# Attention of a two-block sequence model on one core: 1024-column steps, maxima split on POOL and carried through DRAM, scores three steps ahead

## What is computed

```python
q, k, v = (qkv[:, :, 0], qkv[:, :, 1], qkv[:, :, 2])
scale = D ** (-0.5)
scores = jnp.einsum('blhd,bmhd->bhlm', q * scale, k)
attn = jax.nn.softmax(scores, axis=-1)
o = jnp.einsum('bhlm,bmhd->blhd', attn, v).reshape(b, l, c)
```

## Time and profile before

| | |
|---|---|
| runs | 3390.99 us median of 3 (3388.45 to 3393.36) |
| profiled execution, its own time | 3393.34 us |
| its span | 3391.6 us |
| granted PE clock, mean | 0.918 |
| busy: PE, DVE, ACT, POOL | 2929.7, 1827.1, 1464.5, 1628.7 us |
| attention, first `values` to last | 766.2 to 1991.3 us of the span |

### The profile page before, as it was taken

One profiled execution on the slowest core, in us unless ns is written; L12 is line 12 of the kernel. 1 busy time (PEld: TensorE's weight loads), 2 busy tenths in 40 slices (PEclk: granted clock), 3 DMA queues, 4 the chain that ended last, 5 costly groups with the idle time before them and its releaser, 6 DMA issues. The chain is left out here.

```text
span 3391.6 us, 53705 instructions
## 1 busy us (share of the span) xinstructions
PE 2929.7 (86%) x16130; PEld 2357.2 (70%) x16130; DVE 1827.1 (54%) x3056; ACT 1464.5 (43%) x2832; POOL 1628.7 (48%) x1401
## 2 busy tenths in 40 slices
PE   6759899978988889889898967757999999999976
PEld 2147778746656656666565646657999999999975
DVE  3446566568888888888888847760111111111125
ACT  2112222218888888888898842221111111111112
POOL 1232322118888878888888856881222222222210
PEclk8769899979999999999999977878999999999989
DMA  5366565552323323233232234659212112121134
GB/s 163 131 210 209 180 222 201 203 155 55 72 64 76 67 63 78 64 69 72 64 78 64 64 124 175 217 201 305 67 34 67 35 34 67 34 67 34 41 123 159
DMA packets 334756, 373.83 MB, mean 110 GB/s; under 512 B 162577, under 2 KB 226713, under 8 KB 334606
## 3 DMA queue, kind: packets, MB, share of 16 engines
q1 hardware_dynamic: 327128, 359.12, 35.4%
q10 hardware_dynamic: 7482, 12.69, 1.2%
HBM read 221.81 MB, written 149.36 MB: 109 GB/s over the span
## 5 line engine op out<-in xcount | busy, mean ns | idle before, releaser
L754 POOL TENSOR_TENSOR a_pl<-a_pf,a_ph 128x512 fp32r<-128x512 f32 x768 | 1038.4, 1384 | 218.6 <-ACT a_ph L829 218.4
L769 DVE TENSOR_REDUCE a_mx<-a_psum_s 128x1 f32<-128x1024 f32 x512 | 618.5, 1219 | 174.9 <-PE a_psum_s L860 170.1
L829 ACT ACTIVATE a_ph<-a_pf 128x512 fp32r<-128x512 f32 x1024 | 674.7, 659 | 0.0
L824 ACT ACTIVATE a_pf<-a_psum_t 128x512 f32<-128x512 f32 x1024 | 635.3, 621 | 55.1 <-PE a_psum_t L877 53.0
L1433 POOL TENSOR_TENSOR m_al<-m_af,m_ah 128x256 fp32r<-128x256 f32 x288 | 212.4, 737 | 769.2 <-DVE m_ah L1442 769.2
L1481 PE MATMUL m_psum_h<-m_ht,m_w 128*128 128x256 f32 x4032 | 534.8, 284 | 33.4 <-DMA m_w<-w_s 23.0
L1442 DVE CAST m_ah<-m_af 128x256 fp32r<-128x256 f32 x288 | 84.5, 293 | 841.2 <-ACT m_af L1419 841.2
L1481 PEld LDWEIGHTS m_psum_h<-m_ht,m_w 128*128 128x128 f32 x4032 | 509.1, 190 | 37.1 <-issue 35.9
L1495 PE MATMUL m_psum_y<-m_w,m_ah 128*128 128x288 f32 x2304 | 507.1, 297 | 1.4 <-DVE m_y L1459 1.2
L1419 ACT ACTIVATE m_af<-m_psum_h,m_bias 128x256 f32<-128x256 f32 x288 | 137.0, 476 | 818.5 <-PE m_psum_h L1481 818.5
L892 PE MATMUL a_psum_o<-a_ph,a_vs 128*100 128x512 f32 x1024 | 438.6, 428 | 37.9 <-DVE a_pl L802 31.1
(11 more groups left out here) (218 smaller groups left out, 3133.8 us busy)
## 6 DMA issues: line engine op xcount, KB each, us to landing
a_qs<-q_s SPq DMA_DIRECT2D x192, 144.0 KB
a_ks<-k_s SPq DMA_DIRECT2D x192, 144.0 KB
w_s<-q_ws SPq DMA_DIRECT2D x64, 324.0 KB, 3.4
h_s<-p_ht SPq DMA_DIRECT2D x40, 512.0 KB, 5.2
m_ht<-h_s SPq DMA_DIRECT2D x16, 1280.0 KB, 8.4
v_s<-q_vo SPq DMA_DIRECT2D x64, 288.0 KB, 2.3
a_vs<-v_s SPq DMA_DIRECT2D x128, 144.0 KB
q_s<-q_qko SPq DMA_DIRECT2D x32, 512.0 KB, 2.7
```

Of the source, the lines that this page charges most:

```text
L754: pool.tensor_tensor(pl[:, s % RING], pf[:, s % RING], raw(ph[:, s % RING]), ALU.subtract).then_inc(lo_pool, 1)
L769: dve.tensor_reduce(mx[:, u % 2, t:t + 1], p_s[:, bank(u, t)], AX.X, ALU.max) \
L824: act.activation(pf[:, s % RING], p_t[:, s % 2], ACT.Exp, scale=SCALE) \
L829: act.activation(ph[:, s % RING], pf[:, s % RING], ACT.Copy).then_inc(hi_ready, 1)
```

## The change

The attention works in 8 steps of 1024 columns for each head. ACT makes the exponential twice from PSUM (rounded to fp32r, and full), in place of once with a copy. The maxima are split on POOL without a turn, and two DMAs write them to DRAM, element by element; a third DMA reads them back as rows. The rows in `ks` are -1 now, so nothing is negated. `p_s` holds one tile, in place of two, `p_t` two tiles of 1024 columns. The transposed scores go three steps ahead. `finish` is in two parts, with a `max_tile` between them. DVE makes two low parts of 8, reading the full exponential in PSUM.

```diff
-    AHEAD = 5
+    PAIR = 2
+    STEPS = LH * KT // PAIR
+    PER_LH = STEPS // LH
+    COLS = PAIR * GT
+    AHEAD = 3
+    DVE_LO = (1, 5)
-        p_s = ps("s", [P, 2, L])
-        p_t = ps("t", [P, 2, GT])
+        p_s = ps("s", [P, L])
+        p_t = ps("t", [P, 2, COLS])
...
+                def send_max(hd, u):
+                    sp.wait_ge(mh_lo, hd + 1)
+                    for s in range(2):
+                        sp.dma_start(maxima[u, s].rearrange("(t c) -> c t", c=P), raw(mh[:, u % 2, s]),
+                                     allow_slow_non_contiguous=True).then_inc(max_out[u], 16)
                 def put_max(u, i):
-                    sp.wait_ge(s_free[bank(u, KT)], bank_uses(u, i, KT) + 1)
-                    for s in range(2):
-                        sp.dma_start(raw(qs[SROWS + s:SROWS + s + 1, u]).rearrange("o (t c) -> o t c", c=P),
-                                     raw(mxt[:, u % 2, s])).then_inc(max_in[u], 16)
+                    sp.wait_ge(max_out[u], 32 * (i + 1))
+                    sp.dma_start(raw(qs[SROWS:MROWS, u]), maxima[u]).then_inc(max_in[u], 16)
...
                 def body(hd, u, i, last):
                     if not (last and u > 0):
                         sp.wait_ge(p_free, RING + STEPS * hd)
                         load(hd + SLOTS - 1, (u + SLOTS - 1) % SLOTS)
                     if not (last and u == SLOTS - 1):
+                        send_max(hd + 1, (u + 1) % SLOTS)
                         put_max((u + 1) % SLOTS, i + (u + 1) // SLOTS)
...
+                def split_max(hd, u, puts):
...
+                    pool.tensor_copy(mh[:, u % 2, 0], mx[:, u % 2]).then_inc(mh_hi, 1)
+                    pool.wait_ge(mh_hi, hd + 1)
+                    pool.tensor_tensor(mh[:, u % 2, 1], mx[:, u % 2], raw(mh[:, u % 2, 0]), ALU.subtract) \
+                        .then_inc(mh_lo, 1)
...
-                dve.memset(raw(qs[:, 0]), 1.0).then_inc(first_set_up, 1)
...
+                    for k in range(1, STEPS + 1):
+                        over, s = divmod(k, STEPS)
+                        if not (last and u + over >= SLOTS - 2):
+                            max_tile(hd + over + 2, (u + over + 2) % SLOTS, s)
+                        if s + LO_AHEAD in DVE_LO and not (last and u + over == SLOTS):
+                            low(hd + over, s + LO_AHEAD)
+                        if s + LO_AHEAD - STEPS in DVE_LO and not (last and u == SLOTS - 1):
+                            low(hd + 1, s + LO_AHEAD - STEPS)
+                        if (s + 1) % PER_LH == 0:
+                            finish_hi(hd, s // PER_LH)
+                        if s % PER_LH == 0:
+                            finish_lo(hd, s // PER_LH - 1 if s else LH - 1)
...
+                        act.activation(ph[:, s % RING], p_t[:, s % 2], ACT.Exp, scale=SCALE)
+                        full = p_t[:, s % 2] if s in DVE_LO else pf[:, s % RING]
+                        act.activation(full, p_t[:, s % 2], ACT.Exp, scale=SCALE).then_inc(exp_done, 1)
...
+                    if not (isinstance(hd, int) and hd == 0 and t == 0):
+                        pe.wait_ge(s_free, KT * hd + t)
...
+                    if s >= 2 and s - 2 in DVE_LO:
+                        pe.wait_ge(lo_dve, lo_counts(hd, s - 2)[1])
+                    elif not (isinstance(hd, int) and hd == 0 and s < 2):
+                        pe.wait_ge(exp_done, STEPS * hd + s - 1)
...
                         values(hd, u, s)
                         if not (last and u >= SLOTS - 2):
-                            nxt = ((u + 2) % SLOTS, i + (u + 2) // SLOTS)
-                            if s in MAX_STEP:
-                                score_tile(*nxt, MAX_STEP.index(s))
-                            if s == TURN_STEP:
-                                turn(*nxt)
+                            score_tile(hd + 2, (u + 2) % SLOTS, i + (u + 2) // SLOTS, s)
```

More of the change, by code:

```diff
@@ L684, in heads @@
                 body(SLOTS * (n - 1) + u, u, n - 1, True)
[L686 to L692, removed]
         def lo_counts(n_heads, s):
-            d = sum(dve_lo(x) for x in range(s + 1))
+            d = sum(x <= s for x in DVE_LO)
             return NPOOL * n_heads + s + 1 - d, NDVE * n_heads + d
@@ L760, in _, with low, finish_hi, finish_lo @@
             def _(dve):
-                dve.memset(raw(qs[:, 0]), 1.0).then_inc(first_set_up, 1)
                 dve.memset(raw(vs[:, 0]), 1.0).then_inc(first_set_up, 1)
-                dve.memset(raw(qs[:, 1:SLOTS]), 1.0).then_inc(set_up, 1)
                 dve.memset(raw(vs[:, 1:SLOTS]), 1.0).then_inc(set_up, 1)
                 def max_tile(hd, u, t):
[L768 to L782, removed]
+                    if t == 0 and not (isinstance(hd, int) and hd < 2):
+                        dve.wait_ge(mh_lo, hd - 1)
+                    dve.wait_ge(s_ready, KT * hd + t + 1)
+                    dve.tensor_reduce(mx[:, u % 2, t:t + 1], p_s[:], AX.X, ALU.max).then_inc(s_free, 1)
+                def low(hd, s):
+                    dve.wait_ge(exp_done, STEPS * hd + s + 1)
+                    dve.tensor_tensor(pl[:, s % RING], p_t[:, s % 2], raw(ph[:, s % RING]), ALU.subtract) \
+                       .then_inc(lo_dve, 1)
+                def finish_hi(hd, lh):
+                    dve.wait_ge(p_free, RING + STEPS * hd + PER_LH * (lh + 1))
+                    dve.wait_ge(o_out[lh], START + 16 * STORES * hd)
                     dve.tensor_copy(ob[:, lh], p_o[0:VLO, lh]).then_inc(hi_copied, 1)
+                def finish_lo(hd, lh):
                     dve.wait_ge(hi_copied, LH * hd + lh + 1)
@@ L789, in _ @@
                         max_tile(hd, hd, t)
-                    if hd == 0:
-                        turn_lo(0, 0)
+                for s in DVE_LO:
+                    if s < LO_AHEAD:
+                        low(0, s)
+                max_tile(2, 2, 0)
                 def body(hd, u, i, last):
[L794 to L806, removed]
+                    for k in range(1, STEPS + 1):
[10 more added lines that the diff above has]
+                            finish_lo(hd, s // PER_LH - 1 if s else LH - 1)
                 heads(nc.vector, body)
@@ L812, in _ @@
                 set_start(act, o_out + max_in + o_copied)
[L813 to L832, removed]
                 def body(hd, u, i, last):
                     for s in range(STEPS):
[L837 to L844, removed]
+                        act.wait_ge(t_ready, STEPS * hd + s + 1)
+                        act.wait_ge(p_free, STEPS * hd + s + 1)
+                        act.activation(ph[:, s % RING], p_t[:, s % 2], ACT.Exp, scale=SCALE)
+                        full = p_t[:, s % 2] if s in DVE_LO else pf[:, s % RING]
+                        act.activation(full, p_t[:, s % 2], ACT.Exp, scale=SCALE).then_inc(exp_done, 1)
                 heads(nc.scalar, body)
@@ new lines, in scores @@
+                    if s >= 2 and s - 2 in DVE_LO:
+                        pe.wait_ge(lo_dve, lo_counts(hd, s - 2)[1])
+                    elif not (isinstance(hd, int) and hd == 0 and s < 2):
+                        pe.wait_ge(exp_done, STEPS * hd + s - 1)
+                    for r in range(PAIR):
+                        t = PAIR * j + r
+                        m = pe.matmul(p_t[:, s % 2, r * GT:(r + 1) * GT], ks[0:MROWS, u, t * P:(t + 1) * P],
+                                      qs[0:MROWS, u, lh * GT:(lh + 1) * GT], start=True, stop=True)
@@ L890, in values @@
                         pe.wait_ge(lo_pool, n_pool)
-                    out = p_o[0:VW, lh]
-                    pe.matmul(out, vs[:, u, t], ph[:, s % RING], start=(t == 0), stop=False)
-                    m = pe.matmul(out, vs[:, u, t], pl[:, s % RING], start=False, stop=(t == KT - 1))
+                    for r in range(PAIR):
+                        t = PAIR * j + r
+                        cols = slice(r * GT, (r + 1) * GT)
+                        pe.matmul(p_o[0:VW, lh], vs[:, u, t], ph[:, s % RING, cols], start=(t == 0), stop=False)
+                        m = pe.matmul(p_o[0:VW, lh], vs[:, u, t], pl[:, s % RING, cols], start=False,
+                                      stop=(t == KT - 1))
                     m.then_inc(p_free, 1)
@@ L897, in _ @@
                     for t in range(KT):
[L898 to L899 removed]
+                        score_tile(hd, hd, 0, t)
                 for s in range(AHEAD):
@@ L2096, in build @@
     sums = scratch("sums", NHEAD, L)
+    maxima = scratch("maxima", 4, 2, L)
     rsums = scratch("rsums", NHEAD, L)
```

99 lines of the change are left out of this document (43 added, 56 removed).

## The result

| | before | changed |
|---|---|---|
| median of 4 runs | 3389.72 us | 4149.7 us |
| lowest, highest | 3377.27, 3393.36 | 4143.85, 4155.98 |
| profiled execution, its own time | 3393.34 | 4155.98 |
| granted PE clock, mean | 0.918 | 0.855 |
| first to last `values` | 766.2 to 1991.3 | 780.1 to 2755.6 |

The ratio is 1.225, 95% interval 1.2214 to 1.2287: slower, as forecast, but by 760 us where 330 were forecast, and above the upper end of the range (4020).

The account below looks back on a forecast made before the run. No engine alone bounds it; the maxima's DMA chain, already just in time, would set heads at 24.6 us against 19.1. Attention 1225 to 1539 (+314), start +17: 3393 + 331 = 3724, said as 3720; range 3540 to 4020.

Parts of the forecast that it names:

- T0: Reference point of the forecast's times: the end of a head's last `values` on PE.
- 1 add of the second half: DVE's add now stands behind a later tile's maximum: done at T0+4.45, 1.6 us later than before.
- 2 loads through: DMA queue: the same 8 loads stand ahead of the maxima, 8.7 us from the add until empty, T0+13.2.
- 5 fetch landed: `put_max` goes out only after the stores land, into an empty queue: 2.1 us, T0+17.3.
- 6, 7 to the next T0: PE after its 7.4 us idle: 22 matmuls, 5.2 us, plus 2.1 lost to the half clock.
- (4): Completion of the maxima's stores to DRAM: 0.5 us left, bounds 0.3 to 1.3, T0+15.2.
- (3): Two DMAs moving 1024 4-byte elements each to DRAM: 1.5 us, bounds 1.0 to 4.6, T0+14.7.
- rival C: Four-byte stores of maxima are dear: at 60 ns each, head 30.7 us, whole 4090; from 3960 up; 14 in 100.
- Its sign: The two DMAs of maxima showing megabytes per second far below those of the earlier trace's four-byte loads.
- the half clock after the idle time: PE runs at 1.2 GHz for 4.3 us after each head's idle time, losing 2.1 us.
- the start: Before attention, one `p_s` makes and reduces tiles in turn: 16 tiles take 40 us, not 22.6, so +17.
- rival A: Chain of DMAs in attention is not late, engines set the head at 16.5 us: 3238 us; 7 in 100.

Follow-up runs that it names:

- e1: Changed kernel with maxima written to DRAM in runs of 32 bytes, not 4-byte elements, their transposition left out: 3683 us, 1.086 of before.
- e3: Changed kernel with SP sending and fetching the maxima before it issues the loads, 4-byte stores kept: 3849 us, 1.135 of before.
- e4: Changed kernel with the add of a finished half put back right behind its copy on DVE: 4065 us, 1.198 of before.
- e8: Changed kernel's own DMAs, SP's body rotated so maxima go out one head earlier and ahead of the loads: 3616 us, 1.065 of before.
- e13: Changed kernel with maxima through DRAM in 32-byte runs, transposition left out, sent one head earlier ahead of the loads: 3292 us, 0.969 of before.
- e5: Changed kernel with 4-byte elements 64 bytes apart, two further DMAs writing the 32-byte runs read back, transposition left out: 3807 us, 1.122 of before.
- e14: Changed kernel with maxima straight from SBUF to q's rows, 16 DMAs of 128 4-byte elements, sent one head earlier: 3523 us, 1.036 of before.
- e9: Changed kernel with every-eighth-row tiles, maxima straight from SBUF to q's rows in 32-byte runs, sent one head earlier: 3326 us, 0.980 of before.

## Why the prediction was wrong, point by point

| step, us from T0 | forecast | the head above | difference |
|---|---|---|---|
| 1 add of the second half | 4.45 | 5.2 | 0.75 late |
| 2 loads through | 13.2 | 13.8 | |
| 3 elements through | 14.7 | 15.1 | |
| 4 landed, fetch issued | 15.2 | 22.3 | **6.7 over in this step alone** |
| 5 fetch landed | + 2.1 | + 2.2 | 1518.28 to 1520.46 |
| 6, 7 to the next T0 | + 7.3 | + 7.0 | 1520.46 to 1527.42 |
| a head | 24.6 | 31.5 | 6.9 over |

**The step that failed is (4), the completion of the stores to DRAM.** I took 0.5 us, bounded by 0.3 and 1.3 from stores in long runs; it took 7.2. Sixty heads of 6.9 us are 414 us, of the 430 between 3720 and 4150, and e1, which takes away this and the passage of the single elements (3), came to 3683. The bound was too narrow for a reason that could be seen: the earlier trace rows are loads, are stores in long runs, and no row showed a short-run store's landing. I gave that doubt to (3), as a price of moving each element, and rival C said so (60 ns each, 14 in 100, from 3960 up). C has nearly the right time and the wrong place: 128 elements on each engine moved in 1.3 us, 10 ns each, and the queue then stood empty. Its sign, a rate far below that of the earlier trace rows, is not in the profile: 6 or 7 GB/s in most slices, for 1.9 us (head 61), as there.

The rule of the Trainium skill that I weighed ("DMA: Bandwidth & Descriptors", Specifications), that a transfer below 512 bytes is read, modified and written, does not tell these cases apart: runs of 32 bytes are below it too, and SP waited 1.4 us for them.

Another section of that page of the Trainium skill, "Anatomy of one DMA — SWDGE (gpsimd) path", is written for DMAs that GpSimd issues, and these are issued by SP. It says that the semaphore can't be raised until the last byte is confirmed in the target memory, and that a DRAM target can make this surprisingly long. The trace agrees on the place, with 7 us between the last packet and the end of SP's wait. It does not agree on the size: the section gives about 2 us for the whole fixed part, near the 2.1 us that I used from the earlier trace rows, and the two DMAs here needed 11.1 from issue to fetch. The measurement decides.

What held: that SP's order makes one chain out of the add, the store, the loads and the maxima (e3, e4 and e8 each within 24 us of their number); 60 idle times of PE at the first `scores`; the fetch; the half clock after the idle time, 3.4 us of it rather than 4.3 (a window from 1520.4 to 1523.8 has a granted clock of 0.54, the next one 1.00); the durations on POOL and ACT; the start, 14 us against 17. Two smaller sizes were off. PE came to its wait at T0+11.9 and not T0+9.9 (in the head before this one T0 is 1495.27, and the idle time begins at 1507.13), which is why it waits 12.3 us and not 7.4 + 6.9. And the engines' own head was 17.4 us (e13) where I gave 16.5, so rival A's 3238 would have been 3292. What this change's other parts are worth is the difference from there to before: 102 us. The maxima's DMAs as they are, with the order around them, cost 858 (4150 to 3292).

## What to carry to other kernels

A transposition by 4-byte stores to DRAM was paid here in its landing, which the DMA engines' busy share doesn't show: look how close together the writes fall, and prefer a layout in which each partition owns a run. When a DMA is put on a queue, write down all that the same sequencer waits for ahead of it in a period; here the loads and a store's wait belonged to the maxima's way, and another order of the same calls was worth 530 us (e8). Bound a transfer's issue, its packets and its landing separately, each by rows of the same direction and the same run length.

## What the runs showed of the hardware

- Stores of 2048 4-byte elements to DRAM, 16 to each 64 bytes, were through the queue 2.4 us after the issue, and the fetch that waited for their landing went out after 11.1 (head 61). SP waited 8.6 us a head for them, and 2.1 or 1.4 us where they lay 64 bytes apart or in 32-byte runs (e5, e1). To SBUF, a DMA of 128 such elements landed in 2.0 us (e14).
- A weight load of 108 x 128 that reads with a step of 32 bytes took 327 ns (e9), without a step 188 (e13) to 205 (e1).
- A DMA of 128 single elements to SBUF took 0.63 us to issue on SP (e14); one of 128 runs of 32 bytes took 0.57 to SBUF (e9) and 0.41 to DRAM in a quiet queue (e1).
